# First layer of a two-layer decoder: TensorE transposes the gate's rows behind two heads' projections, and takes the gate's product behind the third head's

## What is computed

```python
# attention of layer 0: 16 heads of 128, causal, over a sequence's 64 tokens
h = ln(x)
q, k, v = h @ w_q + b_q, h @ w_k + b_k, h @ w_v + b_v
a = softmax(causal(q @ k.T / sqrt(128)))
x = x + (a @ v) @ w_o + b_o
# the recurrence over time ("wkv"), for which ln(x) is turned to channels x time
x = x + wkv(w, u, ln(x), ctx)
# experts: 16, of which each token takes 4, by the softmax of its gate
xt = ln(x)
scores = softmax(xt @ gate_w.T)          # [tokens, 16]
cw = top 4 experts within the top 2 of 4 groups, weights normalised
x = x + sum_e cw[:, e] * expert_e(xt) + shared(xt)
```

## Time and profile before

| | us |
|---|---|
| median of 3 runs | 1388.76 |
| lowest, highest | 1388.69, 1391.48 |
| the profiled execution's own time | 1389.57 |
| its span | 1387.8 |
| TensorE busy in the span | 1123.2 (81%) |
| VectorE busy in the span | 935.5 (67%) |
| first stage, 60 to 640 us: TensorE busy | 507.93 of 580 |
| the same: VectorE busy | 417.50 of 580 |

### The profile page before, as it was taken

One profiled execution on the slowest core, in us unless ns is written; L12 is line 12 of the kernel. 1 busy time (PEld: TensorE's weight loads), 2 busy tenths in 40 slices (PEclk: granted clock), 3 DMA queues, 4 the chain that ended last, 5 costly groups with the idle time before them and its releaser, 6 DMA issues.

```text
span 1387.8 us, 25403 instructions
## 1 busy us (share of the span) xinstructions
PE 1123.2 (81%) x8276; PEld 970.0 (70%) x8338; DVE 935.5 (67%) x2266; ACT 564.2 (41%) x1990; POOL 535.1 (39%) x575
## 2 busy tenths in 40 slices
PE   6999898888889898955786899996478877777753
PEld 6898898888888787954685699885356655555532
DVE  5756768587867778688663367563367787788753
ACT  5534243332333242413242233332176775667531
POOL 1112122233424343243331465667124355554454
PEclk9999999999999999987798899998689998899765
DMA  5320000101010101015465777675200000000000
GB/s 173 123 69 16 17 24 5 55 13 53 20 47 22 44 24 32 29 35 180 150 182 141 174 131 111 103 116 81 68 17 9 23 17 24 16 17 9 16 18 21
DMA packets 72663, 84.13 MB, mean 61 GB/s; under 512 B 11720, under 2 KB 62632, under 8 KB 72408
## 3 DMA queue, kind: packets, MB, share of 16 engines
q1 hardware_dynamic: 55608, 60.74, 14.7%
q0 software_dynamic: 14592, 19.41, 8.5%
q10 hardware_dynamic: 2336, 2.36, 0.5%
HBM read 49.90 MB, written 32.58 MB: 59 GB/s over the span
## 4 chain that ended last, share of the span: by engine, by line
PE 44%; DVE 27%; DMA 10%; issue 8%; ACT 5%; POOL 4%; SPq 1%; DVEq 0%; POOLq 0%; ACTq 0%
PE bank L514 5%; PE bank L515 5%; PE bank L516 5%; PE bank L1503 4%; PE bank L1969 3%; PE bank L575 3%; DMA xs<-xg,slot 2%; DMA yt<-y_sb,xe 2%; PE bank L1982 2%; PE bank L551 2%; DMA x_sh<-y_sb,xe 2%; DVE k_st L2275 2%; DMA x_sh<-x2e 2%; ACT ex L2101 2%; PE bank L1447 2%
## 5 line engine op out<-in xcount | busy, mean ns | idle before, releaser
L740 ACT ACTIVATE qk<-bank,b_col 128x256 f32<-128x256 f32 x256 | 107.3, 471 | 249.6 <-PE bank L516 247.2
L2101 ACT ACTIVATE ex<-bank,nmx 128x64 f32<-128x64 f32 x512 | 153.4, 337 | 83.3 <-DVE nmx L2285 77.1
L414 POOL TENSOR_TENSOR probs<-shifted,rowinv 64x512 f32<-64x512 f32 x64 | 71.0, 1109 | 275.9 <-DVE rowinv L911 206.7
L514 PE MATMUL bank<-xt_hi,w_hi 128*128 128x256 f32 x512 | 155.4, 304 | 5.3 <-DVE w_lo L875 4.9
L515 PE MATMUL bank<-xt_lo,w_hi 128*128 128x256 f32 x512 | 149.6, 292 | 0.0
L516 PE MATMUL bank<-xt_hi,w_lo 128*128 128x256 f32 x512 | 149.2, 291 | 0.0
L1867 POOL TENSOR_TENSOR k_bd<-k_st,bd_mask 128x512 f32<-128x512 f32 x64 | 67.9, 1063 | 166.0 <-PE bank L1982 147.2
L2101 ACT ACTIVATION_READ_ACCUMULATOR ex<-bank,nmx 128x1 f32 x512 | 117.5, 230 | 0.0
L514 PEld LDWEIGHTS bank<-xt_hi,w_hi 128*128 128x128 f32 x512 | 103.4, 202 | 6.4 <-issue 4.5
L1553 ACT ACTIVATE act_e<-bank 128x176 f32<-128x176 f32 x112 | 35.5, 317 | 172.4 <-PE bank L1449 171.0
L756 ACT ACTIVATE at_hi<-bank,b_col 128x256 fp32r<-128x256 f32 x128 | 53.8, 472 | 126.1 <-PE bank L575 126.1
(11 more groups left out here) (298 smaller groups left out, 3254.3 us busy)
## 6 DMA issues: line engine op xcount, KB each, us to landing
xe<-xs SPq DMA_DIRECT2D x80, 136.0 KB
e_stage<-w_up SPq DMA_DIRECT2D x18, 352.0 KB
terms<-w_qkv SPq DMA_DIRECT2D x12, 512.0 KB, 5.0
down<-w_down SPq DMA_DIRECT2D x16, 176.0 KB
xs<-zero SPq DMA_DIRECT2D x17, 136.0 KB, 1.8
yt<-zero ACTq DMA_DIRECT2D x1, 2176.0 KB, 8.2
xin<-x SPq DMA_DIRECT2D x8, 256.0 KB, 3.0
terms<-w_o SPq DMA_DIRECT2D x4, 512.0 KB, 4.8
```

Source lines behind the costliest of these rows:

```text
L414: pool.tensor_tensor(probs[r, :, SEQ * s:SEQ * s + SEQ], expd[r, :, :], rowinv[r, :].unsqueeze(2).broadcast_to([SEQ, TC * GH, SEQ]), ALU.m ...
L514: nc.tensor.matmul(out, l_hi, r_hi, start=start, stop=False, skip_group_check=True)
L740: ins = nc.scalar.activation(qk[:, par, hh, o, :], p_proj[hh % 2][:, o * TOK:o * TOK + TOK], ACT.Identity, bias=b_col[:, o, h:h + 1])
L2101: ins = nc.scalar.activation(ex[:, g % 2, j, :], p_s[g % 2][:, j * SEQ:j * SEQ + SEQ], ACT.Exp, bias=nmx[:, g % 2, j:j + 1], scale=SCALE1, ...
```

## The change

Two calls are moved in TensorE's list of slot 0, in blocks 2 to 7. No instruction is added or taken out, and no other engine's list changes.

```diff
             transpose_probs(m)
-            if j == 0 and i >= 2:
-                g_transpose(i - 2)
             if more:
 ...
                 project_qk(m + 2, nxt, 0)
                 project_qk(m + 2, nxt, 1)
+            if j == 0 and i >= 2:
+                g_transpose(i - 2)
             if not (last and j == NGRP - 1):
                 scores(m + 1, (j + 1) % 2)
 ...
             mix_values(m, 0, j % 2)
-            if j == 0 and i >= 2:
-                gate(i - 2)
             if j == 2 and i >= 2:
                 rank(i - 2, i + 1 if last else i + 2)
             if more:
                 project_qk(m + 2, nxt, 2)
+            if j == 0 and i >= 2:
+                gate(i - 2)
+            if more:
                 project_qk(m + 2, nxt, 3)
             if j == 0 and not first:
                 k_transpose(i - 1, i + 1)
```

## The result

| | before | after |
|---|---|---|
| median of the first four runs of each, us | 1390.12 | 1375.39 |
| lowest, highest | 1388.69, 1396.86 | 1371.16, 1379.82 |
| the profiled execution's own time | 1389.57 | 1371.16 |
| its span | 1387.8 | 1369.4 |

The ratio of the runs is 0.9871, with a 95% interval of 0.9833 to 0.9908: 1.3% faster, by 12.8 to 23.2 us. A second comparison, with 9 runs of the changed kernel beside 29 of the one before, gave 1378.54 against 1389.83, a ratio of 0.9909 [0.9874, 0.9944]. The forecast was 1373.1 us, within 1367.5 to 1380; both medians lie in the range, 2.3 and 5.4 us above the forecast.

A forecast was written before the change was run, and what follows sets the result against it. TensorE is busiest, but VectorE's list, with GpSimd behind it, was taken to limit slot 0's gain. Six blocks' gains sum to 15.7 us: 1389.6 gives 1373.9, less 0.8 for that execution's excess over the median, 1373.1 us; range 1367.5 to 1380.

The forecast's parts named there:

- TensorE's 32 us: Slot 0, blocks 2 to 7: the most the moved step costs TensorE, 21 us standing and 11 us of slow clock.
- VectorE's list from the gate's rows to `g_soft`: Slot 0: its steps stand end to end once scores are early, so block 3 gains 2.86 us.
- everything comes back: Rival: VectorE and GpSimd have slack in slot 0, so all 32 us are gained, 1356 us; chance 5%.
- The waits: TensorE, slot 0 of block 3: about 1.1 us left at L626, new ones of 1.3 at L597 and 1.3 at L563.
- Its cover: Slot 0, block 3: the later `gate` product is ready at 253.7, 2.4 us before `g_soft` starts at 256.1.
- The hand-over: VectorE, slot 0: the row maximum starts 0.1 us behind the end of `k_apply`.
- The sum: Slot 0, blocks 2 to 7: gains of 3.43, 2.86, 1.81, 3.21, 2.11 and 2.25 us, 15.7 us in all.
- Block 5: Slot 0 of that block: idle time of 2.78 us ahead of the row maximum, so a gain of 3.21 us.
- The clock: Slot 0: the new gaps are shorter than those known to leave either level, so it was priced at nothing.
- the rival in which it falls and stays low: Slot 0: the clock falls, each block loses about 6 us, the kernel takes 1424 us; chance 3%.
- 2.4 us gained: Slot 2, ahead of `project_out`: two low-clock stretches may go; on the other side all six fall low, 4.8 us lost.
- The price of one such stretch: Slot 2: low clock costs 1.2 us, 12 matmuls of `project_out` in 2.9 us instead of 1.7.

The follow-up runs named there:

- e4: The changed kernel with the gate's transposes one step later still, behind the scores; 1378.23 us in one run, slot 0 122.04 us against 120.76.
- e8: The changed kernel with one more discarded reduction of 0.69 us in VectorE's list of slot 0, blocks 2 to 7; 1390.67 us in one run.
- e9: The changed kernel with eight more discarded matmuls (1 us) on TensorE ahead of `k_transpose` in slot 0, blocks 3 to 6; 1381.16 us in one run.
- e1: The kernel before with only the gate's transposes moved, the gate's product left in place; 1378.65 us, ratio 0.9905 to the kernel before.
- e2: The kernel before with only the gate's product moved, behind the third head's projection; 1395.37 us, ratio 1.0052 to the kernel before.
- e6: The changed kernel with GpSimd's `g_rstd` moved ahead of the block's last scatter; 1376.22 us, ratio 0.989 to the kernel before.
- after_again: The changed kernel run once more, unaltered; 1378.54 us, ratio 0.9909 to the kernel before.
- e7: The changed kernel with `g_rstd` ahead of the last scatter and slot 0's probabilities ahead of the first scatter; 1369.99 us, ratio 0.9867 to the kernel before.
- e3: The kernel before with discarded matmuls filling TensorE's wait for the gate's rows, no step moved; 1382.79 us, ratio 0.9967 to the kernel before.
- e7_again: e7 run once more, unaltered, beside e10; 1369.13 us, ratio 0.9829 to the kernel before.
- e10: e7 with 16 discarded matmuls filling the 2.36 us gap ahead of slot 2's second `project_out`, blocks 2 to 6; 1362.65 us, ratio 0.9793 to the kernel before.

## Why the prediction was right

**The bound in slot 0: right, and shown.** The step that carried the forecast was that not TensorE's 32 us but VectorE's list from the gate's rows to `g_soft`, with GpSimd behind it, sets the slot. e4, e8 and e9 show it from three sides: a wait of TensorE filled gives nothing, 0.6 us on VectorE costs 0.6 in five of six blocks, 1 us on TensorE costs 0. The rival "everything comes back" (1356 us) falls with them.

**The waits: right, and of the size given.** For block 3: L626 1.1 us, measured 1.03; L597 1.3, measured 1.03; L563 1.3, measured 1.43. In block 2 L597 waits 0.20 us where 0.5 was forecast, and in block 5 not at all. `gate` costs nothing in its later place (e1). Its cover was forecast as 2.4 us and is 1.8: the product ends at 249.28 and `g_soft` starts at 251.11. In e2, where L626 stays late, there is none, and `g_soft` waits.

**The hand-over: a term too small, in each block.** The sum allowed 0.1 us between `k_apply` and the row maximum. In the trace the row maximum starts at 249.00, 0.08 us *before* the listed end of `k_apply` (248.35 + 0.73). The list from `g_apply` to `g_soft` took 7.54, 7.89, 7.55, 7.66, 7.54 and 8.49 us, about 0.3 less than worked out. That is the excess of 0.29 to 0.37 us in five of the six blocks. This joint makes 0.18 of it in block 3. Another 0.09 stands between the row maximum and `attn_lo`: 1.32 us from start to start (249.00 to 250.32), where the earlier trace rows give 1.41 without the wait (256.18 to 258.13, less 0.54).

**Block 5: mis-sized, 3.21 against 2.10.** The sum let `g_apply` start when it had started before. In this block it came later, since GpSimd's `g_rstd` had to wait for a landing of 4.7 us. The transfers of 385 to 392 us and of 311 to 318 us, blocks 4 and 3, by the list of DMA issues (last number: us to landing):

```profile
x_mid<-x SPq DMA_DIRECT2D x1, 256.0 KB, 4.3
...
xs<-xg,slot POOLq DMA_INDIRECT x1, 4.7
```

```profile
x_mid<-x SPq DMA_DIRECT2D x1, 256.0 KB, 2.8
...
xs<-xg,slot POOLq DMA_INDIRECT x1, 3.2
```

The store of `x_mid` beside it is slow too in the same stretch. GpSimd's wait was 3.81 us where it had been 2.29, and the block gained 1.1 us less. With this wait taken away (e6) block 5 goes from 21.79 to 20.08. Why the landing is slower was not tried. In after_again the rows of block 5 are late too (L626 waits 2.01 us), in e9 they are not. The errors of +0.3 in five blocks and -1.1 in one cancel to 0.45 us of 15.7: that the sum is so close is luck, the closeness in five single blocks is not.

**The clock: right in slot 0 but for block 5, lucky outside it.** Gaps of 1.03 and 1.03 us left it at 1.00 in slot 0 of block 3, and the rival in which it falls and stays low did not come. In block 5 it fell to a mean of 0.79 behind the late rows. Of the clock in slots 2 and 3 the prediction gave "2.4 us gained" as one bound, and 3.2 us came. The price of one such stretch was too small: it was counted over the twelve matmuls of `project_out` (1.2 us), but the clock stays low into slot 3. Against the profile after, block 2 took 1.11 us more in slot 2 and 0.47 in slot 3, block 3 took 1.13 and 0.42, so 1.6 us each. And that both went is a draw: after_again had none of the low stretches either, e1 had three with the same wait ahead of each. This term is larger than all errors in slot 0, and the prediction treated it as a bound only. The Trainium skill, "TensorE: Matmul & The Clock Gate", section "A second HAM failure mode: psum-queue depth-cycling", tells of short idles between groups of matmuls that make the clock swing. By the rows it did not act behind gaps of 1 us in slot 0, but slots 2 and 3 of e6 and e7 look like what it describes, at gaps of 1.9 to 2.4 us.

**The total: near, and partly by luck.** The sum left the clock outside slot 0 and everything behind the first stage at nothing. The profiled first stage ended 19.6 us earlier, not 15.7, while the medians lie 14.7 and 11.3 us apart in the two comparisons. What lies behind the first stage differs from execution to execution by more than these differences, so the 2.3 us between forecast and median say less for the reasoning than the table of slots does.

**What the change's gain is made of** was not split in the prediction. By e3 it is 11.15 us of clock and 5.0 us of overlap, in a change that looks like pure overlap.

**Expectations that failed.** The size of e2 (5.5 us slower in the median, its cause partly open); the time of e3, by 2 us; the start of block 7's rows in e4; the unchanged distance in e6; the totals of e6 and e7 and the ratio of e7_again. The totals left out that the gaps of slots 2 and 3 stay, with whatever low clock comes behind them.

## What to carry to other kernels

Price a moved step by the list of the engine that is next, joint by joint, and not by the idle time that it removes: of 32 us on TensorE 16 came back, and the price by VectorE's list was right to 0.4 us in five of six blocks. Read the granted clock behind every gap: a gap can cost more in what runs slowly behind it than in its own length, and useless matmuls in it can then be a gain. Where a total scatters by more than the effect, measure the stage by the starts of a step that occurs in each round, and use the total only for the verdict.

## What the runs showed of the hardware

**Gaps of one length leave either level of the clock.** Over the 13 profiles other than e10's, a gap of 2.36 us ahead of a `project_out` occurs 78 times, and a stretch of low clock begins at most 1.6 us behind its end in 39 of them; in 14 it holds for at least half of the twelve loads there, in the others it falls mostly on what follows, as in e9. Behind the gaps of 1.5 to 1.9 us ahead of slot 2's products with v it was 5 of 65, all five in block 6, where the gap is longest. Same wait, same work around it, another result in another execution; in e10, with the longer gap filled, none in blocks 2 to 6. One profile therefore does not price such a gap: the changed kernel had none of six twice, e9 five of six.

**The whole time scatters, most of all behind the stage that was changed.** The first stage of the changed kernel repeats to 0.2 us (604.60 and 604.46), that of e7 only to 3.5 (597.40 and 600.90). From there to the end executions took between 763.6 us (before) and 776.7 (e3). Most of it is the experts' stage, up to the first transposes of the second layer, which took 355.5 us (e4) to 367.3 (e7_again) for the same instructions. Such a scatter is enough for the 3 us between medians of the same kernel in two comparisons (1375.39 and 1378.54); what makes it was not tried.
